# A GRU recurrence with a sparse feed-forward behind it, one core: small vector operations moved into the step, one scale for the input weights, row-sized copies

## The chip, the cores and the metric

The kernel runs as one program on one core of a Trainium2 chip. The metric is device time in microseconds (us), the median of several executions. TensorE multiplies matrices (PE in the profile, its weight loads PEld); VectorE (DVE) and ScalarE (ACT) do elementwise work; GpSimd (POOL) and SyncE (SP) issue transfers, and POOL does some bookkeeping. Each engine works through its own instructions in order and waits on semaphores for the others.

## The reference

The input `x` is [16, 256, 512]: 16 sequences, 256 time steps, 512 features. What is computed:

```
xs = swapaxes(inputs, 0, 1)                      # 256 steps of [16, 512]
def cell(h, x):                                  # GRU
    gi = x @ W_ih + b_ih ; gh = h @ W_hh + b_hh
    r = sigmoid(i_r + h_r) ; z = sigmoid(i_z + h_z)
    n = tanh(i_n + r * h_n)
    return (1.0 - z) * n + z * h
hs = scan(cell, initial_state, xs)
scores = einsum('btd,ed->bte', hs, Wg)           # 8 experts, the best 2 are taken
w = softmax of the two best scores, at their experts
y = sum over e of w[..., e] * (silu(hs @ W1[e].T) * (hs @ W2[e].T)) @ W3[e].T   # hidden size 352
return x + y
```

## The kernel before

**Numbers.** Every float32 operand is scaled by a power of two and split into two float16 halves, a high and a low one. A matmul of two such operands is three float16 matmuls. The power of two comes from a sum or a maximum of magnitudes; it is taken across the 128 partitions by two small matmuls (`turn_...` turns the exponents into a row, DVE takes the largest, `spread_...` spreads it). For the four parts of the input weights (`wi`) the maximum is taken by POOL's `partition_all_reduce` instead, for each part by itself, so `gi_inv` has four columns.

**The recurrence.** The loop over `t` (256 steps) stands in full in each engine's program. In a step PE runs `recur(t)`: two passes for the sum of r (L1284 needs the high half of the state, L1290 the low half too), then n, then z (both L1299). Then it runs the other work of the step, in the order that `blocks(t)` gives: exponents turned or spread (P1, P2, X1, X2), a batch of the input projection (`G`, `project`, L1321), rows turned and scored for the routing (`R1`), ranks (`R2`), and from step 52 on (`FIRST`) the feed-forward of one tile of 128 tokens in every four steps. DVE runs `gru_step(t)`: sums the halves of r (`rpre`), n (`hn`), z (`zpre`) out of PSUM, all L1070, forms `rh` and `npre`, and after ACT's tanh and sigmoid `nmh`, `znh`, the high half of the new state (`hlog`, L1094, for which PE's next step waits) and the low half (L1096). ACT does the sigmoids and the tanh, and seeds the PSUM banks of the next step with the input part `gi`.

**Blocks.** Four steps share one block of `gi`. The next block is made in three batches during steps 1, 2 and 3 of four (`BATCHES`, up to block `EARLY` = 12), so one step in four has no batch; from step 48 on there are two larger batches. `take_batch` (L1010) scales a batch and adds the bias: one instruction for each of the four weight parts that the batch touches, two for every batch.

**Behind the step.** All of DVE's other work of step `t` stands behind `gru_step(t)`, that is behind the low half of the new state and ahead of the next `rpre`: the batch, the feed-forward's four operations, `choose`, `take_ranks` and `positions` of the routing (once in eight steps each), `prep(t)` for the eight experts' weights (exponents L960/L961, the largest L964/L965, scales L968/L969, the table `etab` L1040/L1042, and `low`, L1053: the low halves, until step 49), and `x_largest`, `x_scale`, `x_low`, `x_measure` for the next 128 input tokens. ACT has the high halves, magnitudes, `take_rows` and `probabilities` behind its part of the step (`prep`, L766 and L790).

**Transfers.** SP issues the loads of the raw expert weights, each when the place that it goes to is free, the stores of the state rows (`store_rows`, `h_tok`), and in steps 10, 16, 22 and 30 (`OUT_AT`) a quarter of the copy of `x` into the output, DRAM to DRAM, 1024 rows of 2 KB as one contiguous piece. ACT issues a load of `x_raw` in one step of eight. The feed-forward's results are added to the output in DRAM by POOL.

**Ahead of step 0** ACT takes magnitudes of the recurrent and the input weights and makes high halves in alternation; DVE makes the low halves and PE the first block (`project(0)`, `project(1)`).

Of the kernel before, what the change touches and what calls it, by code (L numbers as in the profile page):

```python
# [19 lines left out]
def gru_moe_kernel(nc, x_feat, x_tok, h0_feat, w_hh, b_feat, w_gate, w_units, w_inproj, out):  # L20
# [77 lines left out]
    PIECES = [[(p, max(lo, MW * p), min(hi, MW * p + MW)) for p in range(WI)  # L98
               if max(lo, MW * p) < min(hi, MW * p + MW)] for _, lo, hi, _, _ in BATCHES]
    TAKEN = list(itertools.accumulate(len(p) for p in PIECES))  # L100
    MADE = [sum(b[0] <= i for b in BATCHES) for i in range(BLOCKS)]

    def pieces_upto(i, m):

        order = [(b[0], hi) for b, pieces in zip(BATCHES, PIECES) for _, _, hi in pieces]
        return 1 + min(n for n, (block, hi) in enumerate(order) if block == i and hi >= m)

    def bank_taken(n, bank):

        return max([TAKEN[k] for k in range(n) if BATCHES[k][3] == bank], default=0)  # L110

# [7 lines left out]
    def blocks(t):  # L119
# [13 lines left out]
        if g >= 0 and s in (2, 3):  # L133
            work += [("R1" if s == 2 else "R2", g)]
# [64 lines left out]
    with ExitStack() as ctx:  # L199
# [129 lines left out]
        wi_max_sb = sb("wi_max_sb", [P, WI])  # L329
        wi_pw = sb("wi_pw", [P, WI])  # L330
        wi_sc = sb("wi_sc", [P, WI])
# [7 lines left out]
        gi_inv = sb("gi_inv", [P, 2, WI])  # L339
# [33 lines left out]
        wi_max = sem("wi_max")  # L373
# [16 lines left out]
        prep_scale = sem("prep_scale")  # L390
        prep_hi = sem("prep_hi")
# [75 lines left out]
        ACT_HIGHS = 3  # L467
        N_BIAS, N_CONSTS, N_SETUP = 2, 21, 60
# [4 lines left out]
        def _(sp):  # L473
# [51 lines left out]
            def load_scales(j, v):  # L525
                if j >= 4:
                    sp.wait_ge(ffn_ops, ffn(j - 4, "DOWN_SCALE"))
                elif j == 0:
                    sp.wait_ge(prep_scale, E)
# [29 lines left out]
            for t in range(T):  # L559
# [22 lines left out]
        def _(pool):  # L582
# [137 lines left out]
        def _(act):  # L720
# [30 lines left out]
            def wi_high(p):  # L751
                act.wait_ge(wi_scaled, p + 1)
                S.activation(wih[:, p, 0], wi_raw(p), ACT.Copy, scale=wi_sc[:, p:p + 1]).then_inc(wi_hi, 1)
# [44 lines left out]
            def gi_of(t, gate):  # L798
                i, at = t // BS, t % BS * B
                if t % BS == 0:  # L800
                    act.wait_ge(gi_taken, pieces_upto(i, (gate + 1) * GATE))
# [84 lines left out]
            for k in range(K):  # L886
# [3 lines left out]
                if k:  # L890
                    wi_high(k - 1)
# [11 lines left out]
            for t in range(T):  # L903
# [15 lines left out]
                if t >= GS and t % GS == 3:  # L919
# [629 lines left out]
```

## Time and profile before

| | us |
|---|---|
| median of 3 runs | 1518.22 (1515.42 to 1525.48) |
| the profiled execution, its own time | 1530.83 |
| span of the profiled execution | 1528.8 |
| PE busy | 1416.9 (93%) |
| DVE busy | 1064.6 (70%) |
| ACT busy | 894.2 (58%) |
| POOL busy | 421.8 (28%) |

The profiled execution is 12.6 us above the median of the runs; all that is read from the trace is on its own clock. Times in rows are us from the start of the span, mean durations ns. The clock of PE is given as a share of 2.4 GHz.

### The profile page before, as it was taken

To read this page: it belongs to the slowest core of one execution; us is meant where nothing else is said; L and a number is where in the kernel's file an instruction comes from. 1 tells how busy PE (TensorE), PEld (TensorE's weight loads), DVE (VectorE), ACT (ScalarE), POOL (GpSimd) and SP (SyncE) were. 2 spreads that over 40 slices of the span, in tenths; PEclk is the share of its full clock that TensorE was granted. 3 is DMA by queue.
4 is the path that set the end of the run, shared out by engine and by line. 5 is a ranking of instruction groups with operands and counts; after the bars stand their busy time and mean duration, and the time that the engine had idled before them with its cause. 6 is when DMAs were issued, how large, how long until landed. Compare 5 with 4: busy or idle time off the path is not lost.

```text
span 1528.8 us, 88769 instructions
## 1 busy us (share of the span) xinstructions
PE 1416.9 (93%) x37790; PEld 1237.7 (81%) x37790; DVE 1064.6 (70%) x4246; ACT 894.2 (58%) x2322; POOL 421.8 (28%) x854
## 2 busy tenths in 40 slices
PE   1877787799999999999999999999999999997997
PEld 1877776798888888888888888888888988885664
DVE  6787778777777777777777777777777777763333
ACT  7765576555556555556555556555555655554664
POOL 2001111122332222333322332222333232326343
PEclk9877777889999999999999999999999999998999
DMA  8344422011222212222221222212222212223331
GB/s 289 98 136 133 141 91 55 17 32 39 45 45 39 39 40 44 42 42 45 41 41 41 46 46 38 39 38 46 39 45 46 39 38 46 39 38 72 62 51 16
DMA packets 94979, 88.64 MB, mean 58 GB/s; under 512 B 41343, under 2 KB 74111, under 8 KB 94464
## 3 DMA queue, kind: packets, MB, share of 16 engines
q0 software_dynamic: 17952, 33.64, 12.8%
q1 hardware_dynamic: 73472, 47.75, 10.6%
q8 instruction: 306, 5.01, 1.5%
q10 hardware_dynamic: 3168, 1.57, 0.6%
q14 instruction: 81, 0.66, 0.2%
HBM read 59.12 MB, written 35.72 MB: 62 GB/s over the span
## 4 chain that ended last, share of the span: by engine, by line
PE 84%; DVE 8%; issue 3%; ACT 2%; POOL 1%; DMA 1%; SPq 0%; another core or an unknown queue 0%; DVEq 0%; POOLq 0%; ACTq 0%
PE gn_bank L1299 12%; PE gz_ps L1299 12%; PE b_ps L1321 10%; PE y_ps L1391 9%; PE a_ps L1355 8%; PE b_ps L1355 8%; PE gi_ps L1321 8%; PE gr_ps L1290 6%; PE gr_ps L1284 6%; DVE wexp L1053 2%; PE tr_ps L1369 2%; PE tr_ps L1379 2%; PE tr_ps L1411 1%; DVE gi L1010 1%; ACT rs L809 1%
## 5 line engine op out<-in xcount | busy, mean ns | idle before, releaser
L1299 PE MATMUL gz_ps<-hlog,whh 128*128 128x32 f16 x8192 | 246.2, 177 | 2.7 <-issue 2.7
L1299 PE MATMUL gn_bank<-hlog,whh 128*128 128x32 f16 x8192 | 245.8, 177 | 0.7 <-issue 0.5
L614 POOL DMA_INDIRECT out_y<-work,mt x57 | 94.1, 1651 | 546.0 <-PE gz_ps L1299 307.5
L1299 PEld LDWEIGHTS gz_ps<-hlog,whh 128*128 128x128 f16 x8192 | 224.6, 96 | 3.1 <-issue 3.1
L1299 PEld LDWEIGHTS gn_bank<-hlog,whh 128*128 128x128 f16 x8192 | 224.8, 96 | 1.9 <-issue 1.6
L1321 PE MATMUL b_ps<-xs,wih 128*128 128x64 f16 x4896 | 174.2, 200 | 7.9 <-issue 4.1
L1284 PEld LDWEIGHTS gr_ps<-hlog,whh 128*128 128x128 f16 x4096 | 131.1, 97 | 58.2 <-DVE hlog L1094 38.8
L1284 PE MATMUL gr_ps<-hlog,whh 128*128 128x16 f16 x4096 | 141.7, 170 | 36.1 <-DVE hlog L1094 34.6
L809 ACT ACTIVATE rs<-rpre,sc 128x64 f32<-128x64 f32 x256 | 88.5, 346 | 147.2 <-DVE rpre L1070 144.2
L1321 PEld LDWEIGHTS b_ps<-xs,wih 128*128 128x128 f16 x4896 | 165.2, 103 | 9.4 <-issue 7.1
L1321 PE MATMUL gi_ps<-xs,wih 128*128 128x64 f16 x4320 | 143.8, 195 | 25.0 <-DVE wih L1003 14.5
L1391 PE MATMUL y_ps<-wexp,work 128*128 x639 | 159.1, 382 | 2.0 <-ACT work L844 2.0
L1321 PEld LDWEIGHTS gi_ps<-xs,wih 128*128 128x128 f16 x4320 | 135.5, 99 | 27.2 <-issue 24.1
L1290 PE MATMUL gr_ps<-hlog,whh 128*128 128x32 f16 x4096 | 142.6, 177 | 5.7 <-issue 5.7
L625 POOL DMA_INDIRECT meta<-meta_sb,pos_i x64 | 66.6, 1040 | 225.9 <-PE gn_bank L1299 127.2
L1290 PEld LDWEIGHTS gr_ps<-hlog,whh 128*128 128x128 f16 x4096 | 121.5, 96 | 5.2 <-issue 5.1
L838 ACT ACTIVATE hid<-work,hscale 128x352 f16<-128x352 f32 x71 | 41.8, 588 | 136.4 <-DVE hscale L1156 136.4
L1355 PE MATMUL a_ps<-wexp,xgt 128*128 x732 | 120.6, 314 | 0.4 <-issue 0.4
L1355 PE MATMUL b_ps<-wexp,xgt 128*128 x732 | 119.3, 313 | 0.0
L603 POOL DMA_INDIRECT xgt<-h_tok,mt x52 | 57.0, 1096 | 188.1 <-PE gz_ps L1299 133.5
L1147 DVE SCALAR_TENSOR_TENSOR work<-b_ps,tsc,work 128x352 f32<-128x352 f32 x71 | 41.4, 584 | 93.0 <-PE b_ps L1355 93.0
L1391 PEld LDWEIGHTS y_ps<-wexp,work 128*128 128x128 f16 x639 | 58.8, 99 | 55.3 <-issue 4.1
(201 smaller groups left out, 2651.9 us busy)
## 6 DMA issues: line engine op xcount, KB each, us to landing
wexp<-in_w_units SPq DMA_DIRECT2D x46, 256.0 KB, 3.8
h_tok<-xrow SPq DMA_DIRECT2D x32, 256.0 KB, 2.0
x_raw<-in_x_feat SPq DMA_DIRECT2D x26, 256.0 KB
wexp<-in_w_hh SPq DMA_DIRECT2D x4, 768.0 KB, 7.0
wexp<-in_w_inproj SPq DMA_DIRECT2D x4, 768.0 KB, 12.0
wexp<-in_w_units SPq DMA_DIRECT2D x15, 192.0 KB, 4.7
x_raw<-in_x_feat ACTq DMA_DIRECT2D x6, 256.0 KB
mt<-meta SPq DMA_DIRECT2D x71, 1.0 KB
```

Source lines behind the costliest of these rows:

```text
L603: pool.indirect_dma_start(out=xg[g_slot(j)], out_offset=None, in_=h_tok[0:there * P], in_offset=bass.IndirectOffsetOnAxis(ap=mt[:, j % RIN ...
L614: pool.indirect_dma_start(out=out, out_offset=bass.IndirectOffsetOnAxis(ap=mt[:, j % RING, 0:1].bitcast(I32), axis=0), in_=ysc[y_slot(j)], ...
L625: pool.indirect_dma_start(out=meta, out_offset=bass.IndirectOffsetOnAxis(ap=pos_i[:, i:i + 1], axis=0), in_=meta_sb[:, g, i], in_offset=No ...
L809: S.activation(rs[:], rpre[:], ACT.Sigmoid, scale=scale(SC_INV)).then_inc(sig_r, 1)
L838: S.activation(hid16[:, 0, 0:HE], hid[:], ACT.Copy, scale=hscale[:, 0:1]).then_inc(hid_hi, 1)
L1147: ffn_op(j, "HID", V.scalar_tensor_tensor(out=hid[:], in0=b_ps[:, 0:HE], scalar=inverse(j, 1), in1=hid[:], op0=ALU.mult, op1=ALU.mult))
L1284: pe.matmul(gr_ps[:, j, 0], whh[:, 1, k, j * P:(j + 1) * P], h[:, k, 0], start=False, stop=False, skip_group_check=True)
L1290: mm = pe.matmul(gr_ps[:, j], whh[:, 0, k, j * P:(j + 1) * P], h[:, k], start=False, stop=True, skip_group_check=True)
L1299: mm = pe.matmul(dst[:, j], whh[:, i, k, m * P:(m + 1) * P], h[:, k], start=False, stop=True, skip_group_check=True)
L1321: mm = pe.matmul(BATCH_BANKS[bank][:, (m - first) * BTOK:(m - first + 1) * BTOK], wih[:, p, w_part, (b * K + k) * P:(b * K + k + 1) * P], ...
L1355: mm = pe.matmul(dst, xT[x_slot(j)][:, a * K + k], part[:, k], start=(i == 0 and k == 0), stop=(i == 2 and k == K - 1))
L1391: mm = pe.matmul(y_ps[:], hidT[:, PARTS[i][0] * HB + b], parts[PARTS[i][1]][:, b], start=((i, b) == DOWN[0]), stop=((i, b) == DOWN[-1]))
```

## The change

Five edits:

1. DVE's small operations move into the step. `behind_r(t)` stands between the sums of r and n: the batch of the step before (up to step 48), the expert exponents and scales (one step later than before, each), `x_measure`, `x_largest` and `x_scale` in steps 0, 1, 2 of eight, and in steps 8 to 47 the scores, marks and ranks of the routing. `behind_z(t)` stands behind the sum of z: `etab` and the rest of the choice. Behind the step stay `positions`, the low halves and `x_low`, the feed-forward, and from step 48 on the batches and the routing. The ranks on PE, ACT's `probabilities` and `positions` come one step later in steps 8 to 47.
2. One scale for all input weights: the four magnitudes are waited for, the largest goes through the two small matmuls, POOL's four reductions are gone, `gi_inv` has one column, `take_batch` is one instruction.
3. ACT ahead of step 0: two recurrent high halves instead of three (DVE makes the other two), all four input magnitudes, then the input high halves.
4. DVE ahead of step 0: the five operations for the gate's scale and weights stand behind the first two batches.
5. The wait for the batches of a block stands ahead of `npre` instead of `rpre`; the copies to the output are written as 8 by 128 rows, so that a packet is one row.

```diff
-        if g >= 0 and s in (2, 3):
+        ranked = 4 if t < BS * EARLY else 3
+        if g >= 0 and s in (2, ranked):
             work += [("R1" if s == 2 else "R2", g)]
...
-                    sp.dma_start(out[i * n:(i + 1) * n], x_tok[i * n:(i + 1) * n]).then_inc(out_ready, 16)
+
+                    dst, src = (v[i * n:(i + 1) * n].rearrange("(a b) d -> b a d", b=GS) for v in (out, x_tok))
+                    sp.dma_start(dst, src).then_inc(out_ready, 16)
...
-            for p in range(WI):
-                pool.wait_ge(wi_mag, p + 1)
-                G.partition_all_reduce(wi_max_sb[:, p:p + 1], wi_sum[:, p:p + 1], P, RMAX).then_inc(wi_max, 1)
...
                 wi_magnitude(k)
-                if k:
-                    wi_high(k - 1)
+            for p in range(WI - 1):
+                wi_high(p)
             measure(0, 0)
             wi_high(WI - 1)
...
-                if t >= GS and t % GS == 3:
+                if t >= GS and t % GS == (4 if t < BS * EARLY else 3):
                     probabilities(t // GS - 1)
...
+            def wi_scale():
+                dve.wait_ge(wi_mag, WI)
+                chain(V.tensor_reduce(wi_most[:], wi_sum[:], AX_X, ALU.max))
+                exponents(prep_bits[:, 0:1], prep_exp[:, 0:1], wi_most[:]).then_inc(wi_measured, 1)
+                dve.wait_ge(wi_turned, 1)
+                largest(prep_top, prep_diag, TURNED[0:1], 1).then_inc(wi_topped, 1)
+                dve.wait_ge(wi_spread, 1)
+                scales(wi_pw[:], wi_sc[:], SPREAD[:, 0:1])
                 dve.sem_inc(wi_scaled, 1)
...
-                for p, lo, hi in PIECES[n]:
-                    V.scalar_tensor_tensor(
-                        out=gi[:, i % 2, lo:hi],
...
+                V.scalar_tensor_tensor(
+                    out=gi[:, i % 2, first:last],
+                    in0=BATCH_BANKS[bank][:, 0:(last - first) * BTOK].rearrange("p (m t) -> p m t", t=BTOK),
+                    scalar=gi_inv[:, i // 2 % 2:i // 2 % 2 + 1],
+                    in1=gi_bias[:, first:last].unsqueeze(2).to_broadcast([P, last - first, BTOK]),
+                    op0=ALU.mult, op1=ALU.add).then_inc(gi_taken, 1)
...
-                if t % BS == 0:
-                    dve.wait_ge(gi_taken, pieces_upto(i, M))
                 dve.wait_ge(gh_ready, 3 * t + 1)
                 halves(rpre[:], gr_ps)
+                behind_r(t)
                 dve.wait_ge(gh_ready, 3 * t + 2)
                 halves(hn[:], gn_ps)
                 dve.wait_ge(sig_r, t + 1)
                 after("HN")
                 op(V.tensor_tensor(rh[:], rs[:], hn[:], ALU.mult))
                 after("R_HN")
+                if t % BS == 0:
+                    dve.wait_ge(gi_taken, batches_upto(i, M))
                 op(V.scalar_tensor_tensor(out=npre[:], in0=rh[:], scalar=scale(SC_INV), in1=gi_n,
                                           op0=ALU.mult, op1=ALU.add))
                 dve.wait_ge(gh_ready, 3 * t + 3)
                 halves(zpre[:], gz_ps)
+                behind_z(t)
...
+            def behind_r(t):
+
+                for n in batch_at(t - 1):
+                    if t <= BS * EARLY:
+                        take_batch(n[1])
+                for e in range(E):
+                    s = t - max(MAG_AT[e])
+                    if s == 1:
+                        expert_measure(e)
+                    elif s == 2:
+                        expert_largest(e)
+                    elif s == 3:
+                        expert_scale(e)
+                if t // GS + 1 < UNITS_X:
+                    if t % GS == 0:
+                        x_measure(t // GS + 1)
+                    elif t % GS == 1:
+                        x_largest(t // GS + 1)
+                    elif t % GS == 2:
+                        x_scale(t // GS + 1)
+                g, s = divmod(t - GS, GS)
+                if g >= 0 and t < BS * EARLY:
+                    if s == 3:
+                        rank_scores(g)
+                    elif s == 4:
+                        mark(g)
+                    elif s == 5:
+                        take_ranks(g)
+
+            def behind_z(t):
+
+                for e in range(E):
+                    if t == max(MAG_AT[e]) + 3:
+                        expert_table(e)
+                g, s = divmod(t - GS, GS)
+                if g >= 0 and t < BS * EARLY:
+                    if s == 3:
+                        number(g)
+                    elif s == 4:
+                        pair(g)
...
-                wi_scale(k)
-                if k:
-                    wi_low(k - 1)
-            chain(V.tensor_scalar(gi_inv[:, 0], wi_pw[:], 2.0 ** -28, x_pw[:], ALU.mult, ALU.mult))
+                if k == K - 2:
+                    wi_scale()
+            chain(V.tensor_scalar(gi_inv[:, 0:1], wi_pw[:], 2.0 ** -28, x_pw[:], ALU.mult, ALU.mult))
             assert n_setup[0] == N_SETUP, n_setup
-            wi_low(WI - 1)
+            for p in range(WI):
+                wi_low(p)
             take_batch(0)
             take_batch(1)
-            x_measure(1)
```

## Rows read from the trace of the kernel before

**Rows 1.** Stretches: us, busy of PE, PEld, DVE, ACT, POOL, PE's clock, DMA

```profile
46.20:302.00 255.80, 203.47 (x6454) 196.64 (x6454) 199.58 (x787) 161.02 (x389) 35.62 (x104) 0.79 0.32 92
302.00:1320.00 1018.00, 1011.03 (x28534) 897.15 (x28535) 740.88 (x3052) 584.74 (x1651) 288.55 (x600) 0.99 0.21 41
```

**Rows 2.** Waits from 46.2 to 302: us in total, times, longest

```profile
PE gr_ps L1284 <- DVE hlog L1094: 30.3, 23, 3.2
```

**Rows 3.** Timeline of steps 2 to 5: start, us, what, idle before

```profile
56.45 0.22 DVE L1094 TENSOR_TENSOR hlog<-h_now,znh 128x64 f16<-128x64 f32 x1
...
59.15 1.56 PE L1321 MATMUL b_ps<-xs,wih 128*128 128x64 f16 x48
...
60.45 0.22 DVE L1094 TENSOR_TENSOR hlog<-h_now,znh 128x64 f16<-128x64 f32 x1
...
64.73 0.44 PE L1284 MATMUL gr_ps<-hlog,whh 128*128 128x16 f16 x10 [1.43 <-DVE hlog L1094]
```

**Rows 4.** Timeline of DVE behind step 10 and in step 11

```profile
93.03 0.60 DVE L1010 SCALAR_TENSOR_TENSOR gi<-gi_ps,gi_inv,gi_bias 128x128 f32<-128x128 f32 x2
93.55 0.17 DVE L1106 TENSOR_REDUCE score<-a_ps 128x8 f32<-128x16 f32 x1
...
94.98 0.94 DVE L1053 SCALAR_TENSOR_TENSOR wexp<-wexp,prep_sc 128x704 f16<-128x704 f32 x1
95.84 0.28 DVE L1070 TENSOR_REDUCE rpre<-gr_ps 128x64 f32<-128x128 f32 x1
96.05 0.28 DVE L1070 TENSOR_REDUCE hn<-gn_bank 128x64 f32<-128x128 f32 x1
```

**Rows 5.** Timeline of DVE behind steps 9 and 12

```profile
89.51 0.15 DVE L968 TENSOR_SCALAR x_pw<-gi_ps 128x1 int32<-128x1 f32 x1
...
90.26 0.29 DVE L1070 TENSOR_REDUCE rpre<-gr_ps 128x64 f32<-128x128 f32 x1
...
106.28 0.74 DVE L993 SCALAR_TENSOR_TENSOR xs<-x_raw,x_sc,xs 128x512 f16<-128x512 f32 x1
106.95 0.28 DVE L1070 TENSOR_REDUCE rpre<-gr_ps 128x64 f32<-128x128 f32 x1
```

**Rows 6.** Timeline of PE: a batch at the lower clock

```profile
85.27 2.74 PE L1321 MATMUL b_ps<-xs,wih 128*128 128x64 f16 x48
```

**Rows 7.** The chain that ended last: pieces named issue (start, us)

```profile
96.36 2.92 issue
...
113.04 3.03 issue
...
134.63 1.29 issue
...
166.75 4.42 issue
```

**Rows 8.** Timeline: SP's copies 1 and 3 and first store, ACT in step 14

```profile
91.04 0.64 SPq L566 DMA_DIRECT2D out_y<-in_x_tok  x1
98.89 0.33 SPq L540 DMA_DIRECT2D h_tok<-xrow  x1
...
114.48 0.63 ACT L729 ACTIVATE xrow<-x_raw 128x512 f16<-128x512 f32 x1 [0.89 <-DMA x_raw<-in_x_feat]
...
161.08 0.53 SPq L566 DMA_DIRECT2D out_y<-in_x_tok  x1
```

**Rows 9.** DMA queues from 165 to 166.5, from 145.6 to 146.5, whole span

```profile
q1 hardware_dynamic: 15, 0.98, 162.4%
...
q1 hardware_dynamic: 144, 0.26, 75.3%
...
q0 software_dynamic: 17952, 33.64, 12.8%
```

**Rows 10.** Timeline around step 0: DVE's last low half, ACT's table load

```profile
37.97 1.82 DVE L1003 SCALAR_TENSOR_TENSOR wih<-wexp,wi_sc,wih 128x1536 f16<-128x1536 f32 x1
...
42.27 1.28 ACT L809 ACT_TABLE_LOAD   x1
```

More of the change, by code:

```diff
@@ L97, in gru_moe_kernel, with batches_upto @@
             BATCHES += [(i, 0, HALF, 0, 2), (i, HALF, M, 1, 3)]
[L98 to L100 removed]
     MADE = [sum(b[0] <= i for b in BATCHES) for i in range(BLOCKS)]
[L103 to L106 removed]
+    def batches_upto(i, m):
+        return 1 + min(n for n, b in enumerate(BATCHES) if b[0] == i and b[2] >= m)
     def bank_taken(n, bank):
[L110 removed]
+        return max([k + 1 for k in range(n) if BATCHES[k][3] == bank], default=0)
     def batch_at(t):
@@ L390, in gru_moe_kernel @@
         prep_scale = sem("prep_scale")
+        etab_made = sem("etab_made")
         prep_hi = sem("prep_hi")
@@ L1096, in gru_step, with expert_measure, expert_largest, expert_scale @@
                 op(V.tensor_tensor(parts[:, :, 1], h_now[:, new], parts[:, :, 0], ALU.subtract))
+            def expert_measure(e):
+                dve.wait_ge(prep_mag, 3 * (e + 1))
+                exponents(prep_bits[:], prep_exp[:], prep_sum[:]).then_inc(prep_measured, 1)
+            def expert_largest(e):
+                dve.wait_ge(prep_turned, e + 2)
+                largest(prep_top, prep_diag, TURNED, 3).then_inc(prep_topped, 1)
+            def expert_scale(e):
+                dve.wait_ge(prep_spread, e + 2)
+                if e >= 2:
+                    dve.wait_ge(prep_hi, 3 * (e - 1))
+                    dve.wait_ge(prep_lo, 6 * (e - 1))
+                scales(prep_pw[:], prep_sc[:, e % 2], SPREAD)
+                dve.sem_inc(prep_scale, 1)
@@ L1101, in route_op, with rank_scores @@
                     dve.wait_ge(route_ops, route(g, name))
-            def choose(g):
+            def rank_scores(g):
                 dve.wait_ge(score_mm, g + 1)
@@ L1117, in choose @@
                 route_op(g, "GAP", V.tensor_tensor(gap[:], top[:, 0:1], top[:, 1:2], ALU.subtract), False)
+            def choose(g):
+                rank_scores(g)
+                number(g)
+                mark(g)
+                pair(g)
             def take_ranks(g):
@@ L1244, in _ @@
                         hidden_lo(j)
-                if t >= GS:
-                    g, s = divmod(t - GS, GS)
+                g, s = divmod(t - GS, GS)
+                if g >= 0 and t < BS * EARLY:
+                    if s == 5:
+                        positions(g)
+                elif g >= 0:
                     if s == 2:
@@ L1252, in _ @@
                         positions(g)
-                prep(t)
-                if t // GS + 1 < UNITS_X:
-                    if t % GS == 0:
-                        x_largest(t // GS + 1)
-                    elif t % GS == 1:
-                        x_scale(t // GS + 1)
-                    elif x_low_at(t):
-                        x_low(t // GS + 1)
-                    elif t % GS == 7 and t // GS + 2 < UNITS_X:
-                        x_measure(t // GS + 2)
+                low_halves(t)
+                if t // GS + 1 < UNITS_X and x_low_at(t):
+                    x_low(t // GS + 1)
             choose(LAST)
@@ L1485, in _ @@
             spread_exponents(-1)
+            pe.wait_ge(wi_measured, 1)
+            pe.matmul(TURNED[0:1], prep_exp[:, 0:1], ident[:], start=True, stop=True).then_inc(wi_turned, 1)
+            pe.wait_ge(wi_topped, 1)
+            pe.matmul(SPREAD[:, 0:1], ones[0:1, :], prep_diag[0:1, 0:1], start=True, stop=True).then_inc(wi_spread, 1)
             for n in range(2):
```

101 lines of the change are left out of this document (44 added, 57 removed).

## The prediction

> **What bounds the kernel now.** I began with busy time by stretch [rows 1]. From 302 to 1320 PE is busy 1011.0 of 1018.0 us at a clock of 0.99: nothing that DVE, ACT or the transfers do there can be worth more than the 7 us that are left, and the change gives PE no less work. From 46.2 to 302, steps 1 to 48, PE is busy 203.5 of 255.8 us at a clock of 0.79. This is the stage that the change aims at. Its 52.3 us of idle are of two kinds. The waits show 30.3 us in which PE's first pass of r waits for the state's high half from DVE [rows 2]; the chain shows pieces named issue, in which PE waits for nothing visible, of 1.3 to 4.4 us [rows 7].
>
> Then I took single steps. Step 3 is bare: from one `hlog` to the next 4.00 us [rows 3]. PE fills it, since 48 matmuls of a batch (1.56 us at full clock) stand behind the sum of z and cover DVE's and ACT's chain. A step without a batch (one in four) leaves PE idle for 1.43 us even when DVE is on time [rows 3]. Twelve such steps owe 17.2 of the 30.3 us; 13.1 us are lateness of DVE. More lateness is there, but hidden, because PE was late too: a batch at the lower level of the clock, 1.2 GHz, takes 2.74 us instead of 1.56 [rows 3, 6].
>
> **Part 1, the small operations.** Prices are distances between starts, since DVE's operations overlap [rows 4]: the two-part `take_batch` 0.52 us, the whole `choose` 1.43, a low half 0.86, from `rpre` to `hn` 0.20. `x_scale` 0.75, `x_low` 0.67 [rows 5]. From the same operations I estimate `x_measure` and an expert's exponents at 0.27, a `largest` at 0.44, an expert's scales at 0.40, scores 0.30, marks 0.28, ranks 0.15 (each two to four operations of 0.15 to 0.28). The new `take_batch` is one operation: I take 0.40, between half of the old one and 0.52.
>
> The room: in a bare step DVE is free 0.3 us after `hlog`'s end, r is ready at 1.0 and n at 1.8. Before the change all work beyond 1.3 us ahead of `rpre` makes the step longer, by its excess and 0.2 more, since ACT's sigmoid waits for `rpre`. Step 11 is the example: batch, choice and low half are 2.81 us [rows 4], and `rpre` starts some 2 us after r was ready. After the change one low half (0.86) stays ahead of `rpre`, which then starts at 1.2, and 0.48 us behind `rpre` are free before n is due: a batch alone costs nothing, a batch with `x_scale` 0.67, with `largest` and `x_measure` 0.63. The sigmoid runs meanwhile. Added up over steps 1 to 48 from the schedule, with PE on time, lateness is 42 us before and 28 after. What stays is mostly the doubled low halves of steps 34 to 39, 45 and 47 (1.7 to 1.9 us each), `x_low` and `positions`, which don't move.
>
> Of that gain of 14 us not all arrives, because some of the lateness was hidden. Before, 13.1 of 42 us showed as idle of PE, a third; a third of 14 is 4.5. If steps run at full clock and nothing else holds PE, all 14 arrive. The hidden part also hid behind the stalls of part 3, which go; I take 9, between the ends 4.5 and 14. Behind z, `etab` (about 0.25) and the index (about 0.4) stand in the time in which `nmh` waits for the tanh and `znh` for the sigmoid of z: nothing, at most 0.1 a step if that cover is gone. Waits that are added: `expert_measure` waits for ACT's magnitude with `hn` queued behind it, but ACT must end that magnitude before its own sigmoid, for which `rh` waits anyway; `largest` and the scales wait for matmuls of the step before. `take_batch` no longer waits at the end of a step for a batch that PE is still making. On PE the ranks move to a step without a batch, into its idle time; its wait for `pairs` is over within it. POOL's and ACT's routing comes a step later, and its first user is tile 0 of step 52. From step 48 on the moved work of x stands ahead of `hn` while PE has two batches and the feed-forward to do: nothing.
>
> **The clock.** The granted clock is 0.79 where PE is busy 80% of the time and 0.99 where it is busy 99% [rows 1]. With 15 us of idle gone the share is 85%; on the line between the two the clock is 0.84. Between full and half clock lie 36 batches of 1.18 us, and about 0.15 us in each step, 50 us; a tenth of that is 5. The line may not hold in so small a piece: 3, from 0 to 7.
>
> **Part 2, ahead of step 0.** The last low half of the input weights now ends at 39.8 [rows 10] and PE's last 36 matmuls follow. The new order: ACT makes all four magnitudes by 26.5, DVE's exchange through PE (2.1 us, as that for the recurrent weights) starts behind its third recurrent low half at 27.5, ACT's fourth high half ends at 37.1, the low half behind it at 39.0. That is 0.8 us earlier, but PE has its four parts closer together and may be at the lower clock for longer. I take -0.5, from -1.3 to +1. The five operations behind the second batch (1.1 us) lie beside ACT's table load of 1.28 us [rows 10]; without that cover they cost 0.7.
>
> **Part 3, the copies.** At 165 the queue moves 15 packets with 0.98 MB: 64 KB each, 2.6 us for each on its DMA engine [rows 9]. PE's issue stops for 2.92 us 5.3 us after the first copy was issued, and for 4.42 us 5.7 us after the third [rows 7, 8]; a stop of 1.29 us follows the second. I read these as instruction loads that wait behind large packets, 8.6 us in the three. A packet of one row takes 0.085 us (10.8 us of engine time for the 128 rows of a store) [rows 9], so the queue can be left sooner. But a stop of 3.03 us at 113.04 has no copy near it, only a load of x in 512-byte packets, so small packets are no cure by themselves. I take 6.5 saved, from 8.6 and a little more saved down to 3 lost. The Trainium skill ("DMA: Bandwidth & Descriptors", Queues, rings and completion order) says that a DMA engine changes between queues at packets of some 9 to 17 descriptors; by that a wait behind rows would be shorter than behind one pair of 64 KB pieces, but not as short as one row.
>
> The copy is written as 8 by 128 rows. If it is spread over the eight, each engine carries 128 rows, 10.9 us, instead of two packets, 5.2 us [rows 9]. The same page (Why a DMA increments its semaphore by 16 and not by 1) says that the engines are the largest number up to 16 that divides the slowest dimension, which is 8 here; no trace of before shows such a copy. SP's later loads have tens of us to spare, so the longer copy costs nothing at this rate.
>
> **The sum.** -9 (part 1), -3 (clock), -0.5 (part 2), -6.5 (part 3): -19 us. On the profiled execution's 1530.8 us that is 1511.8; in proportion on the median of the runs, 1518.2, it is 1499.4. With all favourable ends (-14, -7, -1.3, -10) it is -32, 1486. With the unfavourable ones together, -0.5: 1518.
>
> **The rivals.**
> Lateness stays hidden: PE at the lower clock and its own batch of 2.74 us bound the step in 3 of 4 steps, and the reorder shows 4.5 us or less with no gain in clock. For it: a third of the lateness shows now. Against it: 23 waits of PE for DVE, up to 3.2 us long. -11.5 us, 1507.
> The copies aren't what stops the issue, or eight busy engines for twice the time stop it as often. For it the stop at 113; against it the stops behind the first and the third. -12.5 us, 1506.
> PE runs near full clock from early on, and lateness goes in full: -27, 1491.
> Slower: rows copied from DRAM to DRAM through eight engines take far more than a row of a store. POOL's queue, which reads or adds in DRAM, takes 0.174 us for a packet of 1.9 KB [rows 9]. The store of the first state rows is issued at 98.89 behind the copy of 91.04, and ACT's magnitude of step 14, at 114.48, waits for it [rows 8]. So a copy may last 23 us, 0.18 us a row; beyond that the whole chain stands. At 0.35 us a row the first copy ends 21 us too late and the second 11 too late (its magnitude comes six steps after it, not four, at 5.3 us a step [rows 1]: 34 us of room): +32 - 19 = +13 us, 1531; from 0.30 us on the gain is gone.
>
> **How the numbers follow.** A measurement of this kernel can tell about 1% from no change, 15 us. Chances: the forecast 0.42, hidden lateness 0.17, copies without effect 0.15, the fast case 0.21, slower 0.05. The range 1484 to 1512 leaves out the slower case, the worst of the small ones and the best of the fast one. Under 1503 lie the fast case and three quarters or more of the forecast's, and a little of the small ones: 0.6 for faster, 0.36 for the same, 0.04 for slower.
>
> **What would show it.** Right: `hn` starting within 0.2 us of n's end in most steps with one low half; PE's waits for `hlog` near 24 us; a clock above 0.79 up to 302; no stop over 2 us within 12 us of a copy; copies in 2 KB packets; 302 to 1320 unchanged. Wrong: stops at the same places, `hn` late by the batch's operation in every step, ACT's sigmoid waiting for its own high halves rather than for `rpre`, or ACT waiting for a store or a load behind a copy.

## The result, and the profile after

| | before | changed |
|---|---|---|
| median of 10 runs each, us | 1518.62 | 1512.44 |
| range of the runs, us | 1515.07 to 1525.48 | 1507.25 to 1515.01 |
| profiled execution, own time / span, us | 1530.83 / 1528.8 | 1508.42 / 1506.6 |

The ratio is 0.9948, 95% interval 0.993 to 0.9965: 5 to 11 us faster, 7.9 at the ratio. The forecast was 1499.4 us, a gain of 18.8. The profiled executions differ by 22.4 us, because that of before was one of its slower ones (12.2 above its median) and the changed one lay 4.0 below its own.

Stretches of the changed kernel, columns as in [rows 1]: ahead of step 1, steps 1 to 48, steps 49 on, the end.

```profile
0.00:44.80 44.80, 11.20 (x250) 9.96 (x250) 30.25 (x78) 31.69 (x43) 5.85 (x20) 1.00 0.91 285
44.80:287.20 242.40, 198.54 (x6454) 191.35 (x6454) 191.13 (x751) 163.09 (x389) 33.86 (x104) 0.85 0.34 99
287.20:1320.00 1032.80, 1027.05 (x29056) 910.74 (x29057) 737.73 (x3006) 601.45 (x1683) 296.98 (x622) 1.00 0.21 41
1320.00:1507.00 187.00, 170.37 (x2038) 116.04 (x2034) 80.53 (x272) 103.68 (x208) 77.60 (x104) 0.97 0.29 49
```

Steps 1 to 48 take 242.4 us after 255.8 [rows 1]. How far one pair of traces can be read, the later steps show: steps 49 to 255 are 5.2 us shorter too. Over all kernels below they took 1071.8 to 1081.3 us in the old order of DVE's work and 1073.3 to 1086.9 in the new one, so there the change shows no gain. Sizes are therefore taken from medians, and the trace says where.

Waits of the changed kernel from 44.8 to 287.2, columns as in [rows 2]:

```profile
PE gr_ps L1340 <- DVE hlog L1075: 22.1, 24, 1.9
...
PE a_ps L1478 <- DVE pairs L1168: 5.3, 5, 1.5
...
PE gi_ps L1377 <- issue: 5.2, 2, 4.1
...
DVE prep_bits L959 <- ACT xgt L765: 3.6, 2, 2.6
ACT xrow L728 <- DMA x_raw<-in_x_feat: 3.5, 1, 3.5
PE b_ps L1377 <- issue: 3.4, 4, 1.7
...
PE y_ps L1487 <- DVE prep_exp L960: 2.6, 2, 2.1
```

PE's waits for `hlog` fell from 30.3 to 22.1 us [rows 2]. Beside them stand 5.3 us of waits of the moved ranks for `pairs`, in steps without a batch; that PE would have waited for `hlog` there anyway is likely, but not shown. ACT's wait for a load of `x_raw`, 0.89 us in before [rows 8], is 3.5 us here. The chain of the same stretch, its stops and transfers over 1.5 us (answers to [rows 7]):

```profile
95.25 1.72 issue
...
127.58 4.09 issue
...
158.49 1.62 issue
...
187.85 9.01 DMA x_raw<-in_x_feat
```

Step 11 on DVE (answers to [rows 4]):

```profile
91.43 0.23 DVE L1075 TENSOR_TENSOR hlog<-h_now,znh 128x64 f16<-128x64 f32 x1
...
91.96 0.94 DVE L1032 SCALAR_TENSOR_TENSOR wexp<-wexp,prep_sc 128x704 f16<-128x704 f32 x1
92.83 0.28 DVE L1049 TENSOR_REDUCE rpre<-gr_ps 128x64 f32<-128x128 f32 x1
93.03 0.47 DVE L1014 SCALAR_TENSOR_TENSOR gi<-gi_ps,gi_inv,gi_bias 128x256 f32<-128x256 f32 x1
93.42 0.16 DVE L1150 TENSOR_REDUCE score<-a_ps 128x8 f32<-128x16 f32 x1
93.61 0.17 DVE L1152 MAX8 top<-score 128x8 f32<-128x8 f32 x1
93.70 0.27 DVE L1049 TENSOR_REDUCE hn<-gn_bank 128x64 f32<-128x128 f32 x1
```

This is the change as meant. Only a low half (0.87) is left ahead of `rpre`, where 2.81 us stood. Batch and scores stand in the gap, and `hn` starts 2.27 us after `hlog`, 0.23 after n's last matmul ends (at 93.47). The prediction wanted that in most steps with one low half. Of all 48 steps it is so (0.2 us or less beyond the 0.04 that the start takes at best) in 15, and in before it was so in 16.

### The profile page after: what moved, and what is told of

Same layout as the page of the kernel before. It is cut to its first block, busy times and chain, and to the rows that moved or that the text cites. A ratio compares the mean times of both kernels' runs of the same rounds, so it can differ in the third digit from the quotient of the medians.

```text
span 1506.6 us, 88673 instructions
## 1 busy us (share of the span) xinstructions
PE 1407.2 (93%) x37792; PEld 1228.1 (82%) x37792; DVE 1039.6 (69%) x4102; ACT 899.9 (60%) x2321; POOL 414.3 (27%) x850
## 3 DMA queue, kind: packets, MB, share of 16 engines
q8 instruction: 306, 5.01, 1.5%
## 4 chain that ended last, share of the span: by engine, by line
PE 83%; DVE 9%; issue 3%; DMA 2%; ACT 1%; POOL 1%; SPq 0%; DVEq 0%; POOLq 0%; ACTq 0%
PE gn_bank L1355 12%; PE gz_ps L1355 12%; PE b_ps L1377 9%; PE y_ps L1447 9%; PE a_ps L1411 8%; PE b_ps L1411 8%; PE gi_ps L1377 8%; PE gr_ps L1346 6%; PE gr_ps L1340 6%; DVE wexp L1032 2%; PE tr_ps L1425 2%; PE tr_ps L1435 1%; PE tr_ps L1467 1%; DVE npre L1062 1%; DVE gi L1014 1%
## 5 line engine op out<-in xcount | busy, mean ns | idle before, releaser
L1377 PE MATMUL b_ps<-xs,wih 128*128 128x64 f16 x4896 | 168.7, 198 | 4.0 <-issue 3.9
L1377 PEld LDWEIGHTS b_ps<-xs,wih 128*128 128x128 f16 x4896 | 160.3, 101 | 5.1 <-issue 4.2
L1377 PE MATMUL gi_ps<-xs,wih 128*128 128x64 f16 x4320 | 140.7, 194 | 12.2 <-issue 6.9
L1377 PEld LDWEIGHTS gi_ps<-xs,wih 128*128 128x128 f16 x4320 | 133.4, 99 | 13.5 <-issue 13.2
L1049 DVE TENSOR_REDUCE rpre<-gr_ps 128x64 f32<-128x128 f32 x256 | 73.8, 288 | 82.9 <-PE gr_ps L1346 80.9
L794 ACT ACTIVATE gn_bank<-bhn,sc 128x128 f32<-128x128 f32 x256 | 93.5, 365 | 38.5 <-DVE hn L1049 32.2
L1049 DVE TENSOR_REDUCE hn<-gn_bank 128x64 f32<-128x128 f32 x256 | 73.5, 287 | 50.2 <-PE gn_bank L1355 44.4
```

Source lines behind the costliest of these rows:

```text
L794: S.activation(gh[:], values.unsqueeze(2).to_broadcast([P, K, 2, B]), ACT.Copy, scale=scale(SC_SEED)).then_inc(seeded, 1)
L1049: op(V.tensor_reduce(dst, gh[:].rearrange("p k a b -> p k b a"), AX_X, ALU.add))
L1377: mm = pe.matmul(BATCH_BANKS[bank][:, (m - first) * BTOK:(m - first + 1) * BTOK], wih[:, p, w_part, (b * K + k) * P:(b * K + k + 1) * P], ...
```

## Experiments

The kernel before ran beside each group; its medians there were 1521.4, 1527.9, 1532.5, 1526.9 and 1524.5 us. Each group ran on another chip. So ratios are compared, and kernels of one group first. A difference in us is the difference of ratios times before's median of about 1525. "Whole" is a copy of a quarter of x as one contiguous piece, as in before.

### The two parts by themselves

`b_again` is the kernel before, unchanged. 

> The kernel of before once more, unchanged. Theory A (the profiled execution of before was slower than usual, by instruction stops and a low clock in steps 1 to 48, and my sum was made against it): the ratio is 1.00, and a second profile shows steps 1 to 48 in about 246 us, not 255.8, with fewer and shorter stops. Rival B (that profile was typical, and what the change gains in steps 1 to 48 is given back elsewhere): again about 256 us.

`a_whole` is the changed kernel with the old form of the copies, so without part 3:

```diff
-                    dst, src = (v[i * n:(i + 1) * n].rearrange("(a b) d -> b a d", b=GS) for v in (out, x_tok))
-                    sp.dma_start(dst, src).then_inc(out_ready, 16)
+                    sp.dma_start(out[i * n:(i + 1) * n], x_tok[i * n:(i + 1) * n]).then_inc(out_ready, 16)
```

> The changed kernel with the copies in one contiguous piece each, as before. Theory C (rows through eight engines last twice as long, and ACT's loads of x wait behind them): faster than the changed kernel by 3 to 6 us, about 1507, and no wait of ACT for a load of x. Rival D (small packets let instructions pass, so the row copies help by the 6.5 us that I forecast): slower, about 1519. If both are there they cancel: 1512.

`b_rows8` is the kernel before with the new form alone (the same lines the other way round). 

> The kernel of before with the copies alone written as 8 by 128 rows. Theory C: slower by 2 to 4 us than before, since its steps are longer and the loads of x have more time. Rival D: faster by 5 to 8 us, which would be the whole measured gain, the reorder then giving nothing.

`setup_only` has edits 2 to 4 and whole copies, with DVE's small operations behind the step as before: in the changed kernel `behind_r(t)` and `behind_z(t)` are taken out of the step, and

```diff
+                for e in range(E):
+                    s = t - max(MAG_AT[e])
+                    if s == 0:
+                        expert_measure(e)
+                    elif s == 1:
+                        expert_largest(e)
+                    elif s == 2:
+                        expert_scale(e)
+                        expert_table(e)
                 low_halves(t)
...
-        ranked = 4 if t < BS * EARLY else 3
-        if g >= 0 and s in (2, ranked):
+        if g >= 0 and s in (2, 3):
```

> The change without its first edit: one scale for the input weights, one operation for a batch, the new order ahead of step 0, but all small operations of DVE behind the step as before, and the copies in one piece. It parts the gain. Theory E (moving the operations gives most of it, since less of DVE's work is late): 1519, 2 us under before, and the changed kernel with whole copies is 5 us faster than this. Rival F (the shorter batch operation and the earlier step 0 give the gain, the lateness that moves was hidden anyway): 1514, the same as the changed kernel.

Later the changed kernel and its arms ran again, unchanged: 

> The changed kernel once more, unchanged, on the chip of the next three. Ratio to before 0.995, as in the first measurement; it is the base for them.

 

> The changed kernel with whole copies, a second time, now beside the changed kernel on one chip. If the form of the copies is worth nothing (what the row copies save at instruction stops they lose where ACT waits for a load of x): the ratio is within 0.002 of the changed kernel's. If my forecast of 6.5 us for the form was right and the first comparison unlucky: 0.004 higher.

 

> The change without the move of the small operations, whole copies, a second time, on one chip with the next three. Ratio to before 1.000 (0.9997 the first time). The difference of the next run to this one is the move alone.

 

> The changed kernel with whole copies, a third time, beside the version without the move. The move alone: if lateness counts at the 44% that the added operation showed, 14 us of it are 6 us: ratio 0.9965. If the move gives the 12 us that I forecast for it with the clock: 0.992.

| kernel | median, us | ratio to before (95%) |
|---|---|---|
| b_again | 1521.69 | 1.0002 (0.9984 to 1.0021) |
| changed kernel, first / again | 1512.44 / 1526.49 | 0.9948 / 0.9965 (0.9948 to 0.9982) |
| a_whole | 1513.92 | 0.9956 (0.9933 to 0.9978) |
| a_whole_2 | 1528.36 | 0.9974 (0.9953 to 0.9995) |
| a_whole_3 | 1519.9 | 0.9953 (0.9934 to 0.9973) |
| b_rows8 | 1518.53 | 0.9991 (0.9975 to 1.0008) |
| setup_only | 1525.66 | 0.9997 (0.9978 to 1.0016) |
| setup_only_2 | 1527.27 | 0.9994 (0.998 to 1.0008) |

- The new form of the copies: `after_again` against `a_whole_2` on one chip is -0.0009, `b_rows8` against before -0.0009, some 1.4 us each, plus or minus 4.1 and 2.6. Neither tells it from nothing. `a_whole` came out where its two theories cancel (1512), and the interval of `b_rows8` leaves out both of its own, 2 to 4 us slower and 5 to 8 us faster.
- The set-up: -0.0003 and -0.0006, 0.5 to 0.9 us, which alone can't be told from nothing (plus or minus 2 to 3 us). The traces can tell it: step 0 ends at 44.7 to 45.8 us in the kernels with the new set-up and at 45.8 to 46.2 in the others, 0.9 us earlier on the mean.
- The move: `a_whole_3` against `setup_only_2`, one chip, is -0.0041, 6.3 us, plus or minus some 3.7 (0.0020 and 0.0014 taken together). All three `a_whole` against both `setup_only` (means 0.9961 and 0.9996) give 5.3, plus or minus 2.6. Both are near the 5 us of theory E; theory F, that the move gives nothing, is out.

The sum of the three is 7.2 to 8.6 us. The whole change gained 7.9 us the first time and 5.4 the second. So nothing large is missing, and the move is the most of it. `b_again` shows that the trace of before was on the slow side of its kind, as theory A has it, but by less: steps 1 to 48 take 252.2 us, neither 246 nor 256, with the clock at 0.81 and not with fewer stops (17.9 us of them over 1 us, after 15.9).

The traces of the last pair point the same way. First `setup_only_2`, steps 1 to 48, stretch and two lines of its waits (one of them stops of issue):

```profile
45.00:296.20 251.20, 199.63 (x6455) 192.69 (x6455) 194.50 (x750) 160.95 (x389) 35.08 (x104) 0.81 0.32 95
```

```profile
PE gr_ps L1350 <- DVE hlog L1071: 29.9, 23, 3.0
PE b_ps L1387 <- issue: 8.5, 5, 3.7
```

and `a_whole_3`:

```profile
45.70:293.60 247.90, 199.05 (x6455) 192.04 (x6456) 191.30 (x750) 163.28 (x389) 34.10 (x104) 0.83 0.32 95
```

```profile
PE gr_ps L1339 <- DVE hlog L1074: 21.4, 22, 1.9
PE b_ps L1376 <- issue: 11.9, 5, 5.5
PE a_ps L1477 <- DVE pairs L1167: 5.0, 5, 1.4
```

The stretch is 3.3 us shorter, the waits for `hlog` 8.5, and the clock is 0.02 higher, not the 0.05 of the forecast. Over all traces with whole copies steps 1 to 48 take 251.2 to 255.8 us in the old order and 240.7 to 248.4 in the new one.

### What the lateness of n's sum is worth

`low_twice` adds to `a_whole` one operation of 352 columns ahead of `rpre` in 38 steps; its result goes nowhere.

```diff
+                if e < 5 or part == 0:
+                    V.scalar_tensor_tensor(out=again[:], in0=raw_in(e, w)[:, 0:352],
+                                           scalar=prep_sc[:, e % 2, w:w + 1], in1=split_out(e, w, 0)[:, 0:352],
+                                           op0=ALU.mult, op1=ALU.subtract)
```

> The changed kernel with whole copies and one more operation of DVE ahead of the sum of r in each of the 38 steps that have a low half: 352 columns of the low half computed once more into a tile of its own, about 0.52 us each, 20 us in all. By the account of my prediction the lateness of the sum of n grows from 28 to 46 us, by 18. If lateness counts in full: 18 us slower than whole copies; if two thirds of it, as I took: 12; if a third, as the idle of PE in before suggested: 6. This measures the step of my sum from lateness to time.

Measured: 1535.95, 1.003 (1.0013 to 1.0047), against `a_whole_2` in the same group +0.0056, 8.6 us. That is plus or minus 4.1 us, and between the 6 and the 12 that were named for one third and two thirds. By the schedule of the prediction the operation adds 18 us of lateness: 48% of it arrives (the expectation of `a_whole_3` has this share as 44%). The lateness that really stands in the traces is less. It is, in each step, the start of `hn` less the end of n's last matmul, less the 0.04 that it takes at best, summed over steps 1 to 48: 31 to 33 us in kernels with the old order, 22 to 27 with the new one (means 32.0 and 24.3) and 37.0 here, where the other kernels with whole copies and the new order have 23.4 to 23.9. So the schedule gave 14 us of gain in lateness, the traces 8. And of the 13.4 us that `low_twice` adds in the trace, 8.6 or 64% arrive, with all that follows from them, the clock included. Given the interval this share lies between a third and nearly all.

### What the copies cost, and whether their form matters

`b_nocopy` and `a_nocopy` are before and the changed kernel without the copies: x is left out of the output.

```diff
-                    sp.dma_start(out[i * n:(i + 1) * n], x_tok[i * n:(i + 1) * n]).then_inc(out_ready, 16)
+                    pass
...
-                else:
-                    pool.wait_ge(out_ready, 16 * len(OUT_AT))
```

> The kernel of before without the four copies of x into the output (only y is added). Theory G (the copies' price and the reorder are independent): 14 us under before, about 1506, as the same cut gave in the changed kernel (1498.2 against 1513.9). Rival H (while the copies stop PE, DVE catches up, so they hide lateness in before): less than 10 us, 1510 or more would mean 1512, and the reorder is worth more without them.

 

> The changed kernel without the four copies of x into the output: the sum x + y is left out, only y is added into whatever the output holds. It gives the whole price of the copies in their present form. If they cost much (theory C): 8 to 12 us faster than the changed kernel, about 1502; if row packets have made them nearly free (rival D): within 2 us of it.

 

> The kernel of before without the copies, a second time, beside the changed kernel without them. Theory H (the copies' stops hide lateness, so the copies cost before less than they cost the changed kernel): ratio 0.992 to 0.993. Theory G (independent): 0.990.

 

> The changed kernel without the copies, a second time. Theory H: the whole change is worth 12 us without copies, ratio 0.985. Theory G: 6 to 8 us as with copies, 0.985 only if the run before this one gives 0.990.

`a_rows16` has the changed kernel's copies as 16 by 64 rows: `b=16` for `b=GS` in the line above. 

> The changed kernel with the copies as 16 by 64 rows. Theory C (spreading over eight engines doubles the time in which a load of x stands behind the copy): 2 to 4 us faster than the changed kernel and no wait of ACT for a load of x. Rival (it makes no difference how the 2 MB are cut as long as they are issued at once): 1512, with a stop of 3 us or more behind at least one copy.

| kernel | median, us | ratio to before (95%) |
|---|---|---|
| b_nocopy | 1514.93 | 0.9926 (0.9903 to 0.9948) |
| b_nocopy_2 | 1516.39 | 0.992 (0.9901 to 0.994) |
| a_nocopy | 1498.19 | 0.9847 (0.9819 to 0.9874) |
| a_nocopy_2 | 1507.58 | 0.9869 (0.9845 to 0.9894) |
| a_rows16 | 1515.42 | 0.9927 (0.9901 to 0.9953) |

In before the copies cost 11 to 12 us, in the changed kernel with whole copies (mean of three 0.9961, without any 0.9858) 15.7, plus or minus about 3. Theory C had 8 to 12 us for the changed kernel; "nearly free" is out. Before's 11 to 12 lie between theory G (14) and theory H (less than 10); the repeat, 0.992, fits theory H, with the 0.990 of theory G at the edge of its interval. `a_nocopy_2`, its stretch and waits:

```profile
44.90:279.90 235.00, 197.25 (x6455) 189.43 (x6456) 191.04 (x750) 163.04 (x389) 33.99 (x104) 0.85 0.25 66
```

```profile
PE gr_ps L1337 <- DVE hlog L1072: 23.3, 26, 1.9
PE gr_ps L1343 <- issue: 2.2, 1, 2.2
PE b_ps L1374 <- issue: 2.9, 3, 1.9
```

Beside `a_whole_3`, 12.9 us shorter, the waits for `hlog` are no fewer (23.3 and 21.4) and PE is busy 1.8 us less; what is gone is stops, and the clock is 0.02 higher. The chain of `a_whole_3` shows those over 1.5 us, one behind each copy:

```profile
96.13 5.54 issue
...
132.39 1.87 issue
...
161.66 4.39 issue
...
194.09 4.79 issue
```

I added the chain's stops over 1 us from step 1 to 48, in one profiled execution of each kernel:

| copies | kernels | stops over 1 us, sum |
|---|---|---|
| whole | before, b_again, setup_only (2), a_whole (3), low_twice | 11.9 to 17.9, mean 15.8 |
| 8 by 128 rows | changed, changed again, b_rows8 | 8.4, 12.3, 6.9, mean 9.2 |
| 16 by 64 rows | a_rows16 | 8.7 |
| none | b_nocopy (2), a_nocopy (2) | 3.2, 5.5, 3.2, 5.6, mean 4.4 |

Whole less none is 11.4 us: in before the stops are as large as the copies' whole price of 11 to 12. Rows take 6.6 us of them away, near the 6.5 of the forecast, though three traces from 6.9 to 12.3 us don't fix it well.

What the stops wait for can be read from the DMA queues. Queue 8 carries instructions, 306 packets with 5.01 MB, so 16 KB each. 52 of them move in steps 1 to 48, one for some 248 of TensorE's 12908 matmuls and weight loads; no other engine runs nearly as many instructions, so this queue is taken for TensorE's. The first stop of `a_whole_3` lasts from 96.13 to 101.67:

```profile
101.67 0.96 PE L1376 MATMUL b_ps<-xs,wih 128*128 128x64 f16 x15 [5.54 <-issue]
```

From 96.2 to 99.3 packets start on no queue but that of SP's transfers, the copy among them (first row: packets, MB, share of 16 engines). From 99.3 to 99.4 one instruction packet starts (second row):

```profile
q1 hardware_dynamic: 69, 0.63, 59.1%
```

```profile
q8 instruction: 1, 0.02, 58.4%
```

58.4% of 16 engines for 0.1 us is 0.93 us: the packet is there at 100.28, and 1.39 us later TensorE goes on. All 81 stops over 1 us in steps 1 to 48 of the 20 traces end like this, 1.1 to 1.6 us behind the end of a packet of queue 8; a moment picked at random lies so in one case out of ten. So in these stops TensorE waits for its own code. Without copies the packet had started to move before the stop began, in all 10 stops. Of the 18 stops over 3 us with whole copies, 17 have a packet that starts only 1.0 to 3.2 us after the stop began, 16 of them within 7 us of a copy's issue: behind a copy the code comes late. When TensorE asked for it no row shows.

The time that the rows take from the stops is handed back in the step after the fourth copy. The changed kernel, ACT in that step:

```profile
187.85 0.55 ACTq L734 DMA_DIRECT2D x_raw<-in_x_feat  x1
...
191.08 0.35 ACT L808 ACTIVATE rs<-rpre,sc 128x64 f32<-128x64 f32 x1 [1.05 <-DVE rpre L1049]
...
196.89 0.63 ACT L728 ACTIVATE xrow<-x_raw 128x512 f16<-128x512 f32 x1 [3.52 <-DMA x_raw<-in_x_feat]
...
198.99 0.33 ACT L808 ACTIVATE rs<-rpre,sc 128x64 f32<-128x64 f32 x1
```

ACT's sigmoid of the next step comes 7.9 us after the last, where the steps beside it take 4.4 to 4.8. The same wait is 4.6 us in `after_again` and 3.8 in `b_rows8` (and 9.2 and 8.4 us from sigmoid to sigmoid); no trace with whole copies, nor `a_rows16`, shows more than 0.9 us of it at any load, though the load has little room even without copies (1.9 us in step 14 of `b_nocopy_2`). The DMA queues say why. The changed kernel from 189 to 197, DMA engines in tenths and queue 10 (that of ACT's load: packets, MB, share of 16 engines):

```profile
DMA  5555586999965585555554564545555595555555
...
q10 hardware_dynamic: 528, 0.26, 11.8%
```

and `a_rows16` from 191 to 195:

```profile
DMA  9999999999999999998878759221000000000000
...
q10 hardware_dynamic: 528, 0.26, 22.6%
```

With eight rows the copy keeps half of the engines busy at about 200 GB/s, with sixteen nearly all at about 400. (The Trainium skill, "DMA: Bandwidth & Descriptors", Why a DMA increments its semaphore by 16 and not by 1, gives eight engines for this shape; the trace agrees.) The load of x shares the eight with the longer copy. Its packets move from 189.8 to 196.0, 6.2 us (6.2 and 6.6 in the other two), against 1.3 to 4.1 us for the same load in the kernels without that form. About half of its 528 packets are on their way by 191.5, the rest start at 30 to 40 in each half us, among the copy's. Measured over the two steps around the fourth copy, sigmoid to sigmoid, it is 12.3, 14.0 and 12.7 us for eight rows, 12.7 to 13.7 for whole copies in the changed order (10.9 to 13.2 in the old one), and 10.1 for `a_rows16`. Over the five steps 29 to 33 of the changed order it is 27.9 and 29.5 us with eight rows, 28.1 to 28.7 with whole copies, 25.5 with sixteen rows and 23.9 to 24.2 without copies. Stop and wait were exchanged.

`a_rows16` is the test of this: the same packets on all engines, no wait for x, and stops of 8.7 us as with eight rows. It is 0.0030 below the changed kernel (mean of two 0.9957), 4.5 us, plus or minus 4.4 and on another chip: the size of the wait, at the edge of the noise. The sign of its rival, a stop of 3 us or more behind a copy, is there too (3.95 us at 156.2, 5.1 after the third).

### Copies in small pieces

`pieces32` cuts the changed kernel's copy into 32 pieces of 256 KB, one a step, issued when n's sum is ready:

```diff
-    OUT_AT = (10, 16, 22, 30)
+    OUT_AT = tuple(range(10, 42))
...
+                    sp.wait_ge(gh_ready, behind_n(t))
...
-                    dst, src = (v[i * n:(i + 1) * n].rearrange("(a b) d -> b a d", b=GS) for v in (out, x_tok))
+                    dst, src = (v[i * n:(i + 1) * n].rearrange("(a b) d -> b a d", b=16) for v in (out, x_tok))
```

> The changed kernel with the copies in 32 pieces of 128 rows, one in each of the steps 10 to 41, issued when the sum of n of that step is there, over all engines. Theory I (the price comes from 64 KB or 128 rows standing in each engine's queue ahead of an instruction load or a load of x; 8 rows are 0.7 us): 8 to 12 us faster than the changed kernel, about 1502, with no stop over 2 us. Rival J (it comes from the copied bytes themselves, which take DRAM and engine time from all else): as before them, 1511.

 `pieces_late` has them in steps 22 to 53. 

> The changed kernel with the copies in 32 pieces of 128 rows over all engines, in steps 22 to 53 rather than 10 to 41, where fewer expert weights are loaded. Theory K (what the pieces still cost, 5 us against no copies, is their meeting with the weight loads in steps 10 to 28): 2 to 4 us faster than the pieces in steps 10 to 41, ratio 0.986. Rival (each piece costs its bit anywhere, and in steps 49 to 53 PE has no idle time to hide it in): 0.988 to 0.990.

 Once more: 

> The changed kernel with the copies in 32 pieces in steps 10 to 41, a second time. If spreading the copies is what pays: ratio to before 0.988 to 0.990, 8 us or more under the changed kernel's 0.9957 (the mean of its two). If the first measurement was lucky: 0.993.

 And in the kernel before: 

> The kernel of before with the same 32 pieces and nothing else. No copies at all gave it 0.9923. If spreading gets back most of that price there too: 0.994 to 0.996, without any part of the change under study. If the pieces only pay where DVE is early: 0.998 or more.

| kernel | median, us | ratio to before (95%) | stops over 1 us |
|---|---|---|---|
| pieces32 | 1509.93 | 0.9881 (0.9857 to 0.9904) | 6.4 |
| pieces32_2 | 1508.51 | 0.9921 (0.989 to 0.9952) | 6.1 |
| pieces_late | 1516.68 | 0.9907 (0.9885 to 0.9928) | 6.3 |
| b_pieces32 | 1516.33 | 0.9963 (0.9947 to 0.9979) | 1.6, and ACT waits 2.8 for x |

The chain of `pieces32_2` keeps two stops over 1 us, at the steps where the kernels without copies have theirs (131.29 and 154.84 in `a_nocopy_2`):

```profile
130.85 2.30 issue
...
155.35 3.78 issue
```

Against the mean of the whole copies (0.9961) the stops fall by some 9 us and the time by 0.0060 (mean of `pieces32` and its repeat 0.9901), 9 us, as theory I has it. Its "no stop over 2 us" did not come true: 2.19 and 2.39 in `pieces32`, 2.30 and 3.78 above. `pieces_late` is no better than the pieces in steps 10 to 41, so meeting the weight loads is not what the pieces still cost (theory K is out). `b_pieces32` gains 5.6 us, plus or minus 2.4, about half of the copies' price in before, without any part of the change under study. `pieces32` is the best kernel of the study that computes the whole output, about 15 us below before and 7 to 10 below the changed one.

## Why the prediction was wrong

**What bounds the kernel**: right in kind. Everything that moved lies in steps 1 to 48, in waits for `hlog` and in stops.

**Part 1 and the clock**: direction right, size half. The forecast was -9 and -3; measured are 6.3 together, plus or minus 3.7, or 5.3 over all pairs. The failed term is "lateness is 42 us before and 28 after": in traces it is 31 to 33 and 22 to 27, so 8 us go, not 14. The error is mostly in the 42, which was added up "with PE on time". PE wasn't, with a clock of 0.79 and its stops; that this is the reason is likely, but not shown. The step from lateness to time was nearer. The forecast let 12 of 14 us arrive, clock included, 86%; `low_twice` has 64% of the trace's lateness, and 8 by 0.64 is 5.1. The clock was counted from an execution at 0.79; four others with the old order and copies have 0.81 to 0.82 and the changed order 0.83 to 0.85, so 0.02 to 0.03 was to be had, not 0.05. The rival "lateness stays hidden" (4.5 us or less, no gain in clock) was nearer in size. Its ground, one third of 14 us, is not what happened: more than a third arrives, of fewer us, and the clock does rise.

One added wait was dismissed too fast: "ACT must end that magnitude before its own sigmoid". That is so, but the magnitude can itself be late, and `hn` is then queued behind the wait. The changed kernel, steps 31 and 33:

```profile
199.11 0.17 DVE L959 TENSOR_SCALAR prep_bits<-prep_sum 128x3 int32<-128x3 int32 x1 [2.62 <-ACT xgt L765]
199.39 0.28 DVE L1049 TENSOR_REDUCE hn<-gn_bank 128x64 f32<-128x128 f32 x1
...
207.98 0.28 DVE L1049 TENSOR_REDUCE rpre<-gr_ps 128x64 f32<-128x128 f32 x1
...
209.50 0.20 DVE L959 TENSOR_SCALAR prep_bits<-prep_sum 128x3 int32<-128x3 int32 x1 [0.97 <-ACT xgt L765]
...
210.25 0.27 DVE L1049 TENSOR_REDUCE hn<-gn_bank 128x64 f32<-128x128 f32 x1
```

In step 31 ACT's magnitude stood behind its wait for x, and `hn` comes 2.8 us late (3.6 in `after_again`, 0.1 in `a_whole`). In step 33 `hn` starts 2.27 us after `rpre`, 1.5 late. That is no new cost: in before DVE waits 0.7 us for the same magnitude, and `hn` of step 33 comes 1.8 late. But the move didn't win it either.

**Part 2**: right, 0.5 to 0.9 us against 0.5, with the earlier end of step 0 in the traces behind it.

**Part 3**: this step failed. "6.5 saved" was right for the stops (6.6), they are tied to the copies, and TensorE waits in them for instructions, as the prediction read them from [rows 7, 8]. Wrong was "SP's later loads have tens of us to spare, so the longer copy costs nothing at this rate": it looked at SP's queue alone. ACT's own load of x, on a queue of its own, shares the eight engines, and ACT wants it 5.5 us after the issue; 3.5 to 4.6 us of wait stand there. By stops and waits some 2 to 3 us should be left; the medians show 1.4, plus or minus 2.6 and 4.1, and cannot tell that from 3. "ACT waiting for a load behind a copy" stood in the list of what would show it wrong, and it did; the stop of 4.09 at 127.58, 9 us after the second copy was issued, did too.

**302 to 1320 unchanged**: right within 0.5%. The 5 us that the pair shows are within what these steps vary from trace to trace, 1071.8 to 1086.9.

**The sum**: 12 + 0.5 + 6.5 became 5.3 to 6.3, 0.5 to 0.9 and 1.4. The rivals "hidden" and "copies without effect" were each given about one chance in six as if only one could happen. In size both nearly did: 4.5 and 0.5 alone are a gain of 5, 1513. In mechanism neither did as written, since the copies are what stops the issue, and rows do shorten the stops; the wait for x is what made them worth so little. That two parts could both fall short belonged in the range, whose upper end of 1512 left it out.

**Left open**: whether the stops hide lateness. The change gains 0.0039 with whole copies, 0.0065 without any and 0.0062 with pieces (means; 6, 10 and 9 us), which points that way, but the differences have an uncertainty about as large as themselves. Also open is why the instruction packets start late behind a copy, since no row shows when they are asked for. That TensorE's stops are waits for code follows from where their ends lie, not from a run that changed the code. The Trainium skill ("Runtime: NRT & Kernel Launch", Instruction fetch mechanics) has instruction code fetched in blocks over a DMA queue of its own, its cost mostly hidden; the trace agrees on blocks (16 KB) and queue, but here stops of up to 5.5 us are not hidden.

## What to carry to other kernels

When a large transfer is reshaped, ask for every queue which short load with little room shares its DMA engines, not only what is queued behind it; a copy with much time to spare is best cut into small pieces spread over the steps. Moving small operations off a chain is worth the lateness that the trace shows, not the one that a schedule gives, times the share that arrives, and one kernel with the lateness raised measures that share. Rivals that touch different parts of a change can all come true, so the forecast needs their joint case.

## What the runs showed that was not expected

- Four copies of 2 MB in the background cost 11 to 16 us in steps that use no result of theirs, most of it as stops of TensorE's issue (15.8 against 4.4 us), each of which ends 1.1 to 1.6 us behind a 16 KB packet of instructions. In 2 KB packets the stops are 9.2, in 256 KB pieces 6.3.
- A copy of 8 by 128 rows runs at about 200 GB/s and stretches a 256 KB load to over 6 us; the same bytes as 16 by 64 rows run at about 400.
- The unchanged kernel of before gave medians from 1518.6 to 1532.5 us in six groups of runs, the last five each on another chip, a spread larger than the effect measured here.
